# A graph layer on one core: the attention's norm vectors are folded into its weights, rows are normalized by ScalarE, and the node value and output bias are added in the mixing

## The reference

```
xn = layernorm(x)                                  # rows, no gain, no shift
g  = segment_sum(w_e * xn[src_e], dst_e) + node_value[:, None]
q, k, v = xn wq^T, xn wk^T, xn wv^T                # 4 heads of 64
k = layernorm(k per head) * kg + kb ;  v = layernorm(v per head) * vg + vb
kv[h] = sum over nodes of k[h]^T v[h] / N          # 64 x 64 per head
mix = concat_h(q[h] kv[h]) wo^T + bo
x  = x + g + mix
x  = x + experts(layernorm(x))                     # top 2 of 8 experts, 256 -> 512 -> 256
```

## Time and profile before

| | |
|---|---|
| median of 3 runs | 2285.6 us (2284.03 to 2287.64) |
| profiled execution | 2287.49 us, span 2285.7 us |
| busy over the span | PE 92%, DVE 86%, POOL 71%, ACT 52% |
| front | 0 to about 178 us |
| eight sort rounds with the mixing | 178 to about 301 us |
| last issue of a gather | 1796 us |

### The profile page before, as it was taken

How to read it: one execution, slowest core, us unless ns; L and a number is a source line. 1 busy time by engine, 2 the same in 40 slices (tenths; PEclk the granted TensorE clock), 3 DMA queues, 4 the chain that set the end, 5 groups by cost and what they waited for, 6 DMA issues and landing times. The chain is left out here.

```text
span 2285.7 us, 45562 instructions
## 1 busy us (share of the span) xinstructions
PE 2101.8 (92%) x16549; PEld 1849.5 (81%) x16550; DVE 1958.9 (86%) x3342; ACT 1177.3 (52%) x1696; POOL 1613.5 (71%) x1364
## 2 busy tenths in 40 slices
PE   7996789999999999999999999999999728999993
PEld 4665678888888888888888888888789618999992
DVE  7998999999999999999999999999778595555552
ACT  2225655555545555555554555554223157888771
POOL 3770067777777777777777777777777347888873
PEclk9997999999999999999999999999999868999996
DMA  4542433333223333332233233332445454555555
GB/s 140 156 121 76 129 113 91 91 89 102 89 90 100 93 93 90 102 94 92 91 102 90 89 90 101 93 92 87 133 130 155 155 140 78 82 83 81 82 81 140
DMA packets 160929, 235.87 MB, mean 103 GB/s; under 512 B 54834, under 2 KB 121805, under 8 KB 160490
## 3 DMA queue, kind: packets, MB, share of 16 engines
q0 software_dynamic: 70896, 164.43, 27.9%
q1 hardware_dynamic: 75536, 55.29, 8.4%
q10 hardware_dynamic: 14314, 13.68, 1.8%
HBM read 186.46 MB, written 53.24 MB: 105 GB/s over the span
## 5 line engine op out<-in xcount | busy, mean ns | idle before, releaser
L816 POOL DMA_INDIRECT picked<-xn_dram,place x1029 | 1185.8, 1152 | 435.6 <-issue 302.5
L914 PE MATMUL bank<-picked,pick_w 128*128 128x256 f32 x2058 | 504.1, 381 | 16.4 <-DMA picked<-xn_dram,place 15.8
L1026 ACT COPY stage<-bank 128x512 f32<-128x512 f32 x343 | 200.9, 586 | 548.4 <-PE bank L902 542.5
L914 PEld LDWEIGHTS bank<-picked,pick_w 128*128 128x128 f32 x2058 | 386.5, 190 | 85.4 <-issue 34.9
L910 PE MATMUL bank<-window,stage 128*128 128x256 f32 x1568 | 382.7, 387 | 0.0
L1287 DVE TENSOR_TENSOR hot_w<-hots,cur 128x1536 bf16<-128x1536 bf16 x343 | 328.6, 958 | 11.9
L980 ACT COPY field_rep<-fields 128x1666 bf16<-128x1666 bf16 (+1 forms) x193 | 322.4, 1675 | 1.2 <-DVE vals L1163 1.2
L910 PEld LDWEIGHTS bank<-window,stage 128*128 128x128 f32 x1568 | 283.6, 191 | 30.7
L1283 DVE TENSOR_TENSOR hots<-ends,cur 128x1408 bf16<-128x1408 bf16 x343 | 303.4, 885 | 1.7 <-ACT cur L1020 1.7
L902 PE MATMUL bank<-hot_w,hots 128*128 128x128 bf16 x4116 | 285.9, 219 | 4.4 <-issue 3.5
L910 PE MATMUL bank<-stage 128*128 128x256 f32 x1176 | 286.0, 386 | 0.0
(11 more groups left out here) (255 smaller groups left out, 3386.7 us busy)
## 6 DMA issues: line engine op xcount, KB each, us to landing
picked<-xn_dram,place POOLq DMA_INDIRECT x1029
w<-in_L_ffn_W_dram SPq DMA_DIRECT2D x16, 512.0 KB, 10.0
xn_dram<-xn ACTq DMA_DIRECT2D x49, 128.0 KB, 1.9
xT_dram<-xT ACTq DMA_DIRECT2D x49, 128.0 KB, 2.1
base_dram<-acc SPq DMA_DIRECT2D x7, 896.0 KB, 7.8
sum_dram<-acc SPq DMA_DIRECT2D x7, 896.0 KB, 4.6
z_dram<-vals SPq DMA_DIRECT2D x7, 896.0 KB, 8.5
out_dram<-sum_dram SPq DMA_DIRECT2D x1, 6250.0 KB, 21.8
```

The costliest lines, as they stand in the source:

```text
L816: pool.indirect_dma_start(out=picked[:, i % SETS * PICK + q, :], out_offset=None, in_=xn_dram, in_offset=bass.IndirectOffsetOnAxis(ap=plac ...
L914: mm = pe.matmul(sum_ps[pp], pick_w[i % SETS][:, q, :], picked[:, i % SETS * PICK + q, :], start=False, stop=(q == PICK - 1))
L1026: act.copy(block_sb[pp].rearrange("p j c -> p (j c)"), banks[pp][:, :]).then_inc(a_copied, 1)
```

## The change

- The affine parts of the two norms go into weights. With a basis matrix per norm (`basis`, made by DVE in iterations 6 and 7 from `ones_at`, `spread_of` and the four vectors), PE multiplies wo and wq by them (iterations 9 and 12), ACT copies the first (`take_wo`), DVE the second (`center_wq`). A centered head has a sum of zero, so its last column is redundant: `hat` holds a 1 there, and the plain product of values and keys, two matmuls of 128 columns per tile, carries the sums as well. The two one-column matmuls go, and so do `key_sums` and most of `kv`.
- `normalize` moves from DVE to ACT, as scale and bias of one activation, behind `take_xT`; `xn` has four rooms instead of three. POOL makes `center` = -mean * rstd per chunk.
- `shift` goes. The node value joins `add_mix` (one instruction with two additions). The output bias joins the mixing matmul: a normalized row has the sum zero, so feature 0 of each row can be given by the others; the weights of feature 0 are taken from all others (`first_dim`), row 0 of `xT` is set to ones once in each room (by POOL), and row 0 of M becomes bo.
- So `load_xT` may not write over row 0 of the first half: it becomes two loads, one of partitions 1 to 127, one of partition 0, second half.
- The four vectors are loaded by eight small loads of 64 partitions ahead of the windows, instead of four behind them.

```diff
 (front)
+            def normalize(t):                      # ACT; before: DVE tensor_scalar
+                ...
+                act.activation(xn[t % ROOMS][:, :], acc[:, t, :], ACT.Identity, bias=center[c % 2][:, i:i + 1], scale=rstd[c % 2][:, i:i + 1]).then_inc(xn_done, 1)
...
-                    pe.matmul(kv_ps[c][:, 0:P + 1], hat[t % 2][0:rows, 2 + c, 0:P], hat[t % 2][0:rows, c, :], ...)
-                    mm = pe.matmul(kv_ps[c][:, P + 1:P + 2], hat[t % 2][0:rows, c, 0:P], hat[t % 2][0:rows, c, P:P + 1], ...)
+                    mm = pe.matmul(kv_ps[c], values, keys, start=(t == 0 and c == 0), stop=(t == LAST), skip_group_check=True)
...
-            def shift(t):
-                dve.scalar_tensor_tensor(out=acc[:, t, :], in0=acc[:, t, :], scalar=nv[:, t:t + 1], in1=bo_b[:, :], op0=ALU.add, op1=ALU.add)
 (edge_sum)
             def load_xT(c):
                 of = xT_dram[at, :].rearrange("(t p) c -> p t c", p=P)
-                to = picked[:, 0:BU, :] if c % 2 else stage[:, 0:BU * D].rearrange("p (t d) -> p t d", d=D)
-                sp.dma_start(to, of).then_inc(xT_in[c % 2], 16)
+                to = xT_room[c % 2]
+                sp.dma_start(to[1:P, :, :], of[1:P, :, :]).then_inc(xT_in[c % 2], 16)
+                sp.dma_start(to[0:1, :, P:D], of[0:1, :, P:D]).then_inc(xT_in[c % 2], 16)
...
+            for i in range(2):
+                pool.memset(xT_room[i][0:1, :, 0:P], 1.0).then_inc(small_in, 16)
...
+                    if m == 0:
+                        pe.matmul(mix_ps[m], ident[0:1, :], bo_row[0:1, :], start=False, stop=True)
...
-                dve.tensor_tensor(acc[:, t, :], acc[:, t, :], mix_ps[t % 4], ALU.add).then_inc(mix_added, 1)
+                dve.scalar_tensor_tensor(out=acc[:, t, :], in0=acc[:, t, :], scalar=nv[:, t:t + 1], in1=mix_ps[t % 4], op0=ALU.add, op1=ALU.add).then_inc(mix_added, 1)
...
-            key_sums()
+            kv()        # four tensor_scalar of 64 x 64; the rest of the old kv() is gone
             hot_tiles(0)
```

More of the change, by code:

```diff
@@ L231, in front @@
         rstd = [sb(f"rstd{i}", [P, UN]) for i in range(2)]
+        center = [sb(f"center{i}", [P, UN]) for i in range(2)]
         hsum = sb("hsum", [P, 2, HH])
@@ L278, in _ @@
             matrix(w_nat[:, 2, :, :], wo, w_in[1])
-            matrix(mixing["wq"], wq, w_in[1])
+            matrix(wqA, wq, w_in[1])
+            with nc.allow_non_contiguous_dma(reason="one value per partition"):
+                for i, v in enumerate((kg, kb, vg, vb)):
+                    for h in range(P // HD):
+                        sp.dma_start(col[h * HD:(h + 1) * HD, i:i + 1], v.rearrange("(d a) -> d a", a=1)).then_inc(w_in[1], 16)
             for n in range(NT):
@@ L287, in _ @@
                 window(n)
[L288 to L292, removed]
+            for i in range(ROOMS):
+                sp.wait_ge(stored[i], 16 * ((NT + ROOMS - 1 - i) // ROOMS))
             for i in range(DEPTH):
-                sp.wait_ge(stored[i], 16 * ((NT + DEPTH - 1 - i) // DEPTH))
                 sp.wait_ge(xT_out[i], 16 * ((NT + DEPTH - 1 - i) // DEPTH))
@@ L367, in repeat_sample, with take_wo @@
                 act.copy(tile_rep[:, at, :], tile_s[:, at].unsqueeze(2).broadcast_to([SP_P, CUT, G])).then_inc(repeated, 1)
+            def take_wo(n):
+                act.wait_ge(w_turned, n + 3)
+                act.copy(woT[:, :, :].rearrange("p k d -> p (k d)"), side_ps[:, :]).then_inc(w_ready, 1)
+            for t in range(ROOMS):
+                normalize(t)
             for t in range(DEPTH):
@@ L413, in kv_product @@
                 for c in range(2):
[L414 to L417, removed]
+                    keys, values = (hat[t % 2][0:rows, at:at + P // HD, :].rearrange("p h d -> p (h d)") for at in (c * (P // HD), H + c * (P // HD)))
+                    mm = pe.matmul(kv_ps[c], values, keys, start=(t == 0 and c == 0), stop=(t == LAST), skip_group_check=True)
                 mm.then_inc(kv_used, 1)
@@ L447, in _ @@
                     last.then_inc(w_turned, 1)
+                if t == 9:
+                    pe.wait_ge(w_ready, 6)
+                    for c in range(2):
+                        mm = pe.matmul(side_ps[:, c * D:(c + 1) * D], basis[1][:, :], woT[:, c, :], start=(c == 0), stop=(c == 1), skip_group_check=True)
+                    mm.then_inc(w_turned, 1)
+                if t == 12:
+                    pe.wait_ge(w_ready, 7)
+                    for c in range(2):
+                        mm = pe.matmul(side_ps[:, c * D:(c + 1) * D], basis[0][:, :], wqA[:, c, :], start=(c == 0), stop=(c == 1), skip_group_check=True)
+                    mm.then_inc(w_turned, 1)
             kv_product(LAST)
@@ L514, in begin_at, with center_wq @@
                 dve.tensor_scalar(starts[:, :], start_f[:, :], 0.0, float(E - SC), ALU.max, ALU.min).then_inc(starts_done, 1)
[L516 to L528, removed]
-            def shift(t):
-                dve.scalar_tensor_tensor(out=acc[:, t, :], in0=acc[:, t, :], scalar=nv[:, t:t + 1], in1=bo_b[:, :], op0=ALU.add, op1=ALU.add)
+            def center_wq():
+                dve.wait_ge(w_turned, 5)
+                then(dve.tensor_copy(first_dim[:, :], side_ps[:, :].rearrange("p (k d) -> p k d", d=D)[:, :, 0]))
+                for k in range(2):
+                    dve.tensor_scalar(wqA[:, k, :], side_ps[:, k * D:(k + 1) * D], first_dim[:, k:k + 1], None, ALU.subtract)
             def apart(c, m):
@@ L603, in _ @@
             weights()
-            for t in range(DEPTH):
-                normalize(t)
             small()
-            for t in range(DEPTH):
-                shift(t)
             for t in range(NT):
```

166 lines of the change are left out of this document (79 added, 87 removed).

## The result

The changed kernel takes 2485.4 us (median of 4 executions, 2477.5 to 2485.7), the kernel before 2284.8 (4 executions, 2280.9 to 2287.6). The ratio is 1.085, 95% interval 1.083 to 1.087: 8.5% slower. The profiled execution took 2485.4 us, its span is 2483.6.

The account below looks back on a forecast made before the run. PE bounds the main loop, DVE the sort rounds, a PE-ACT loop and the window loads the front. The slow xT loads shift the span, 2285.7 + 177.5 = 2463.2, + 1.8 - 1.9 = 2463 us; range 2436 to 2493.

Parts of the forecast that it names:

- The load of xT: First mixing: 127 partitions use one DMA engine, 37.9 us a load, first add of chunk 6 +177.5 us; chance 0.78.
- Rival A: First mixing: wg, bg and bias do not wait behind the big xT loads; +162 us, time 2448; chance 0.12.
- Rival B: xT load still spreads over the engines, so the other terms stand: -5.9 us, time 2280; chance 0.07.
- C: xT loads spread, but window loads are issued no earlier: +1.6 us, time 2287; chance 0.03.
- Front, -7.5: Stage before the sort rounds: earlier window loads and a shorter tail make it 7.5 us shorter.
- first term: Start of the front: earlier first xn on ACT and hats no longer late start the window loads 5.7 us earlier.
- The tail's 1.8: End of the front: PE follows the last window at once and kv_product is shorter, 1.8 us for both.
- ACT's normalize, cost 0: Front: normalizing on ACT takes 0.5 us a tile, hidden in idle queue time; cost 0, without this cover 24 us.
- add_mix, +3.2: Mixing on DVE: each of 49 adds goes from 414 to 479 ns, +3.2 us in all.
- Making M, -1.6: Before the mixing: most of kv() falls away, so DVE starts when its input is there, -1.6 us.

Follow-up runs that it names:

- before127: The kernel before with only its xT column load cut into partitions [1:128] and partition 0; 2701.4 us in one execution, kernel before 2541.6.
- two_engines: The changed kernel with the xT column load cut into 122 partitions, partitions [1:6] and row 0; 2589.7 us in one execution, kernel before 2541.6.
- three_engines: The changed kernel with the xT column load cut into 123 partitions, partitions [1:5] and row 0; 2541.1 us in one execution, kernel before 2541.6.
- small_first: The changed kernel, 127-partition loads kept, with wg, bg and bias loaded before the first two xT column loads; 2465.6 us in one execution.
- split112: The changed kernel with the xT column load cut into 112 partitions, 15 partitions and row 0; ratio to the kernel before 1.0013, timed again 1.0005.
- before_sample_late: The kernel before, with ScalarE issuing the sample's load after the five loads that TensorE's first transposes wait for; ratio 0.9997.
- sample_late_timed: split112 with the load of the sample of destinations issued only after the first two weights landed; 2527.1 us, kernel before 2537.5, ratio 0.9971.
- before_sample_early: The kernel before with the two small loads of kg and kb moved behind the sample's load; 2562.8 us in one execution, kernel before 2538.7.

## Why the prediction was right, and by how much it was off

*The load of xT: right.* One engine, 24 GB/s, loads one after another, a period of 40.3 forecast and 40.95 measured, the main loop shifted as a block. before127 shows that this alone makes the loss of the mixing, two_engines and three_engines that the divisor does.

*Where 22.4 us more came from* (2463 forecast, 2485.4 measured). At the first add of chunk 6 the forecast had 470.3, the profile 482.9, 12.6 more: 2.8 from the start of edge_sum (170.8 forecast, 173.6), 3.5 up to the first add of chunk 0, 0.9 in its seven adds, 1.8 from the third load's issue to its add, 2.0 in three periods of 40.95 and 1.6 in the last. For the 3.5, the semaphores of the changed kernel's loads say more: load 1 has landed at 253.9, 80.3 us after the first issue (78.4 forecast), bias 1.7 us later (1.4 forecast), and the first add comes another 2.2 us later (0.9 forecast), TensorE being at granted clock 0.50. So 1.9, 0.3 and 1.3. One reason was wrong here although its time was nearly right: I let the small loads queue behind load 1, but SP could not even issue them before that load was nearly over. Of the rest, 0.5 lies up to the main loop, 5.1 in it (1492.8 from first to last `hots`, 1487.7 before), 2.3 behind it, and 1.9 is my correction from the profiled execution to the median, which here did not apply. The 5.1 is not explained. It may be of that occasion, since the four profiles of the second one, small_first with its 127 partitions among them, have 1485.0 to 1487.8; it is not one odd execution, since three of the changed kernel's four agree within 0.4 us.

*Rival A (small loads not held up).* Its condition is what small_first makes true. A was priced 15 us below the forecast; small_first is 14.6 us below the changed kernel at the first add of chunk 6 (17.7 counted from the first issue).

*Rival B and C (the load spreads).* split112 is their case: 1.0013 and, on the steadier occasion, 1.0005. C, with its lost gain of the front, is nearer than B.

*Front, -7.5: failed in its first term.* "The window loads start 5.7 us earlier" assumed that the weights land when they did before. They landed 4.5 us later, and the first window load came at 46.95, not near 40. With the sample's load held back it is at 40.61 and 39.92, forecast 40.3, and edge_sum begins at 169.5 and 169.0, forecast 170.8. That looks like the forecast, but the weights come at 9.16 there, 2.4 us sooner than in the kernel before, which the forecast did not have. Against before_sample_late, whose weights are as early, the first window load gains 2.3 to 3.2 us (43.10 to 40.82, 40.61 and 39.92). So the two mechanisms (first xn on ScalarE beside the weights, hats no longer late) are worth about half of the 5.7, and the order of two DMA queues, which the edit touched in passing, took them back. That edge_sum still began 4.7 us earlier was luck: "the front ends a fixed time after its first window load" does not hold either, since the stream of window loads takes 106 to 111 us in the thirteen profiles, and the changed kernel's was the shortest. The tail's 1.8 is borne out: from the last window load's issue to edge_sum it is 21.4 to 22.8 us in the four profiles of the old front, 19.5 to 21.1 in the nine of the new one.

*ACT's normalize, cost 0.* 600 ns, not 500 (49 times, 585 to 602). The loop of PE and ACT stays at 2.93 us a tile: the normalizing lies in ACT's wait for the next projection.

```profile
100.32 0.60 ACT L375 ACTIVATE sq<-bank 128x512 f32<-128x512 f32 x1 [1.01 <-PE bank L431]
...
100.82 0.37 ACT L365 COPY xT<-bank 128x256 f32<-128x256 f32 x1
...
101.64 0.60 ACT L358 ACTIVATE xn<-acc,center,rstd 128x256 f32<-128x256 f32 x1 [0.46 <-ACT xT L365]
...
103.26 0.60 ACT L375 ACTIVATE sq<-bank 128x512 f32<-128x512 f32 x1 [1.01 <-PE bank L431]
```

Of the 2.07 us that ACT had to wait per tile, 1.01 and 0.46 are left.

*add_mix, +3.2.* 0.060 us an add instead of 0.065, 2.9 in all. As forecast it does not count here, where DVE waits for the loads; in split112 it does. *Making M, -1.6.* From the first xT issue to the first add 28.75 us before, 29.22 in split112_again, 27.62 in split112, 27.7 in sample_late_timed: between +0.5 and -1.1, where -1.6 was forecast.

## What to carry to other kernels

Before a DMA's row range is changed, even by one row, ask into how many engines the new count divides: [1:128] for [0:128] made loads of 2.6 us into loads of 38, and [16:128] beside [1:16] costs 1 us of issue instead. A load that is slow holds its queue and may hold the engine that issues, so small loads that something waits for go ahead of it. When loads are removed or moved at the start of a program, look at what moves up: here the gain in the front hung on whether a 781 KB load that nobody needed for 20 us came before 256 KB of weights.

## What the runs showed of the hardware that I had not expected

- SP's issue of a 3.5 KB load behind a load on one engine lasted 34.8 to 38.6 us in the changed kernel (43.2 for the last). With loads on two engines the pair of issues of a load took 15 to 20 us, on three 9 to 12, and with 112 partitions 0.9 to 1.0.
- A load of 0.2 KB behind the sample's 781 KB on one queue landed 14.5 us after its issue (before_sample_early), and the same load of 125 partitions, issued 0.6 us sooner on ScalarE's queue, made the last five increments of 256 KB on SP's queue 4.4 us later.
- The main loop took 1485 to 1493 us on two occasions and 1699 to 1751 on three, one of them on the same chip, while the mixing kept its durations. In split112 TensorE stands for 1.2 us at a time, with nothing in the profile to wait for, and then its granted clock falls to 0.50 (here at 344):

```profile
341.71 0.27 PE L880 MATMUL bank<-hot_t,before 128*128 128x49 bf16 x4 [0.93 <-issue]
343.14 0.26 PE L880 MATMUL bank<-hot_t,before 128*128 128x49 bf16 x4 [1.16 <-issue]
344.57 1.12 PE L880 MATMUL bank<-hot_t,before 128*128 128x49 bf16 x23 [1.17 <-issue]
```

  Idle time of that kind adds up to 133 us in its main loop, and 236 us run at half clock, which costs at most another 118 (an estimate). Together they are of the size of the 264 us by which that loop is longer. What makes the stops is open.
